# Flamingo-style gated block on one Trainium2 core: the router projection with the gate stationary and the token columns moving

## The reference

```python
# cross part: k = v = ctx, q = layernorm(x), heads of 8 channels
kv = einsum('bhil,bhjl->bijhl', k_, v_)
y = irfft(rfft(kv, 2L) * rfft(ssm_kernel, 2L))[..., :L]     # causal convolution of length 1024
out = einsum('bijhl,bhil->bjhl', y + kv * D, q_)
x = x + tanh(g_xattn[0]) * out
# expert part, n = layernorm(x), tokens are the 4096 rows of 1024
scores = softmax(n @ G)            # G is (1024, 8): the router projection
value, indices = top_k(scores, 2)
x = x + tanh(g_ffn[0]) * sum over the 2 experts of value * (down(silu(gate n) * up n) + lora)
```

## Time and profile before

| what | value |
|---|---|
| median of 3 runs | 1568.64 us (1567.76 to 1572.28) |
| the profiled execution | 1570.3 us, span 1568.5 us |
| mean granted TensorE clock | 0.965 of full |
| TensorE busy | 1426.0 us, 91% |
| TensorE weight loads busy | 1380.1 us, 88% |
| VectorE busy | 1148.1 us, 73% |
| ScalarE busy | 774.6 us, 49% |
| GpSimd busy | 1177.9 us, 75% |

### The profile page before, as it was taken

How to read it: one execution, slowest core, us unless ns; L and a number is a source line. 1 busy time by engine, 2 the same in 40 slices (tenths; PEclk the granted TensorE clock), 3 DMA queues, 4 the chain that set the end, 5 groups by cost and what they waited for, 6 DMA issues and landing times. The chain is left out here.

```text
span 1568.5 us, 33155 instructions
## 1 busy us (share of the span) xinstructions
PE 1426.0 (91%) x10482; PEld 1380.1 (88%) x10483; DVE 1148.1 (73%) x1913; ACT 774.6 (49%) x1359; POOL 1177.9 (75%) x765
## 2 busy tenths in 40 slices
PE   4999999999999999999999999545998988989994
PEld 4999999999999999999999999445988877888883
DVE  3999999999999999999999999582444444444442
ACT  5665656656665565566657565102333333333331
POOL 6989888898988989889898887043656566565664
PEclk9999999999999999999999999657999999999997
DMA  5766667676676766767666675164999999999996
GB/s 193 229 201 226 203 216 223 208 231 201 215 225 207 227 200 223 217 207 229 207 221 211 209 227 187 53 196 109 174 224 222 199 214 229 196 215 230 170 171 88
DMA packets 124431, 314.97 MB, mean 201 GB/s; under 512 B 26160, under 2 KB 26672, under 8 KB 124400
## 3 DMA queue, kind: packets, MB, share of 16 engines
q1 hardware_dynamic: 93728, 239.83, 49.6%
q0 software_dynamic: 30672, 74.75, 24.4%
HBM read 215.37 MB, written 100.73 MB: 202 GB/s over the span
## 5 line engine op out<-in xcount | busy, mean ns | idle before, releaser
L532 DVE TENSOR_REDUCE oT<-z 128x128 f32<-128x1280 f32 x256 | 380.6, 1487 | 7.8
L633 PE MATMUL Y<-kvhi,t_hi 128*128 128x288 f32 x1280 | 382.6, 299 | 0.0
L634 PE MATMUL Y<-kvlo,t_hi 128*128 128x288 f32 x1280 | 377.8, 295 | 0.0
L635 PE MATMUL Y<-kvhi,t_lo 128*128 128x288 f32 x1280 | 377.1, 295 | 0.0
L1081 POOL DMA_INDIRECT out<-made,dest x142 | 222.3, 1566 | 164.6 <-DMA out<-made,dest 115.4
L307 POOL TENSOR_TENSOR kvlo<-kv,kvhi 128x1152 fp32r<-128x1152 f32 x128 | 340.7, 2683 | 0.0
L290 POOL TENSOR_TENSOR kv<-cT 128x768 f32<-128x768 f32 x128 | 236.5, 1847 | 8.4 <-DMA cT<-in_c 8.4
L634 PEld LDWEIGHTS Y<-kvlo,t_hi 128*128 128x128 f32 x1280 | 241.0, 188 | 0.0
L635 PEld LDWEIGHTS Y<-kvhi,t_lo 128*128 128x128 f32 x1280 | 241.0, 188 | 0.0
L633 PEld LDWEIGHTS Y<-kvhi,t_hi 128*128 128x128 f32 x1280 | 240.7, 188 | 0.0
L515 DVE TENSOR_TENSOR z<-Y,qT 128x512 f32<-128x512 f32 x256 | 176.9, 691 | 50.6 <-PE Y L635 41.8
(11 more groups left out here) (162 smaller groups left out, 3337.9 us busy)
## 6 DMA issues: line engine op xcount, KB each, us to landing
cT<-in_c SPq DMA_DIRECT2D x32, 768.0 KB, 8.1
t_hi<-khi SPq DMA_DIRECT2D x64, 384.0 KB, 3.8
t_lo<-klo SPq DMA_DIRECT2D x64, 384.0 KB, 5.0
u_hi<-kshi SPq DMA_DIRECT2D x64, 320.0 KB, 5.9
u_lo<-kslo SPq DMA_DIRECT2D x64, 320.0 KB, 6.9
x_nat<-in_x SPq DMA_DIRECT2D x32, 512.0 KB, 4.2
out<-x_new SPq DMA_DIRECT2D x32, 512.0 KB, 4.9
normed<-n SPq DMA_DIRECT2D x32, 512.0 KB, 7.6
```

What stands on the lines that cost most here:

```text
L532: nc.vector.tensor_reduce(oT[p][:, 2 * r:2 * r + 2, h * IB:(h + 1) * IB], view(z[s][:], [[ZC, 2], [2, IB], [2 * IB, ZS], [1, 2]]), AX.XY, ...
L633: nc.tensor.matmul(out, w_hi[:, w], m_hi[:, c, :], start=start, stop=False)
L634: nc.tensor.matmul(out, w_hi[:, w], m_lo[:, c, :], start=False, stop=False)
L635: return nc.tensor.matmul(out, w_lo[:, w], m_hi[:, c, :], start=False, stop=stop)
```

## The change

The gate becomes the stationary operand: 128 x 16, its high and its low 8 columns. The high and the low part of the transposed tokens lie beside each other in `n2_parts` and move together, 256 columns for each of the 8 blocks of the model dimension. The result is 16 x 256 in the first bank of XP: rows are gate columns, columns are high and low tokens. ScalarE copies it into `gated`, whose other 112 rows have been set to zero once. A new step on TensorE, `turn`, transposes the two halves of `gated` into the second bank of XP, and VectorE sums for each token and expert the four terms. The product of the two low parts, which the old form leaves out, is now in the sum. `turn(i - 2)` stands in TensorE's list after `shared(i, 1)`, and VectorE's `take_lr` moves from before to after the fourth `total` of head 0.

```diff
-        n2_hi, n2_lo = sb("n2_hi", [P, NC, P], F32R), sb("n2_lo", [P, NC, P], F32R)
+        n2_parts = sb("n2_parts", [P, NC, 2, P], F32R)
-        p_small = sb("p_small", [P, E])
+        gated = sb("gated", [P, 2 * P])
...
                 def take_small(i):
                     eng.wait_ge(ag_ready, i + 1)
-                    if not (isinstance(i, int) and i < 1):
-                        eng.wait_ge(lr_done, i)
-                    nc.scalar.copy(p_small[:], XP[:, E:2 * E]).then_inc(small_done, 1)
+                    if isinstance(i, int) and i < 1:
+                        eng.wait_ge(gated_zero, 1)
+                    else:
+                        eng.wait_ge(turned, i)
+                    nc.scalar.copy(gated[0:2 * E, :], XP[0:2 * E, 0:2 * P]).then_inc(small_done, 1)
...
                 def take_lr(i):
-                    eng.wait_ge(ag_ready, i + 1)
+                    eng.wait_ge(turned, i + 1)
                     at = slice(i, i + 1) if isinstance(i, int) else bass.ds(i, 1)
                     to = logits[:, at, :].rearrange("p o n -> p (o n)")
-                    eng.wait_ge(small_done, i + 1)
-                    nc.vector.tensor_tensor(to, XP[:, 0:E], p_small[:], ALU.add).then_inc(lr_done, 1)
-
-
+                    nc.vector.tensor_reduce(to, view(XP[:], [[1, E], [P, 2], [E, 2]], HALF), AX.XY, ALU.add).then_inc(lr_done, 1)
+
+
+                nc.vector.memset(gated[:], 0.0).then_inc(gated_zero, 1)
...
                     multiply(i, p, 0, 3)
+                    total(i, p, 0, 3)
                     if not (isinstance(i, int) and i < 2):
                         take_lr(i - 2)
-                    total(i, p, 0, 3)
...
                     for c in range(NC):
 
-                        nc.tensor.matmul(XP[:, 0:2 * E], n2_hi[:, c, :], ag_parts[:, c].rearrange("p o n -> p (o n)"),
-                                         start=c == 0, stop=False)
-                        mm = nc.tensor.matmul(XP[:, 0:E], n2_lo[:, c, :], ag_parts[:, c, 0, :], start=False, stop=c == NC - 1)
+                        mm = nc.tensor.matmul(XP[0:2 * E, 0:2 * P], ag_parts[:, c].rearrange("p o n -> p (o n)"),
+                                              n2_parts[:, c].rearrange("p o n -> p (o n)"), start=c == 0, stop=c == NC - 1)
                     mm.then_inc(ag_ready, 1)
+
+                def turn(i):
+                    eng.wait_ge(small_done, i + 1)
+                    for half in range(2):
+                        mm = nc.tensor.transpose(XP[:, HALF + half * P:HALF + (half + 1) * P],
+                                                 gated[:, half * P:(half + 1) * P], ident[:])
+                    mm.then_inc(turned, 1)
...
                     conv(i, 0, 3)
                     shared(i, 1)
+                    if not (isinstance(i, int) and i < 2):
+                        turn(i - 2)
                     conv(i, 1, 0)
...
                 project(NT - 2)
+                turn(NT - 2)
                 transpose_n2(NT - 1, 1)
                 project(NT - 1)
+                turn(NT - 1)
```

More of the change, by code:

```diff
@@ L179, in attend @@
         lr_done = sem("lr_done")
+        turned = sem("turned")
+        gated_zero = sem("gated_zero")
         w_in, whi_done, wlo_done, w_out = sem("w_in"), sem("whi_done"), sem("wlo_done"), sem("w_out")
@@ L442, in high_n2 @@
                         eng.wait_ge(ag_ready, i)
-                    nc.scalar.copy(n2_hi[:], XP[:].rearrange("p (c n) -> p c n", c=NC)).then_inc(n2hi_done, 1)
+                    nc.scalar.copy(n2_parts[:, :, 0, :], XP[:].rearrange("p (c n) -> p c n", c=NC)).then_inc(n2hi_done, 1)
                 def take_small(i):
                     eng.wait_ge(ag_ready, i + 1)
-                    if not (isinstance(i, int) and i < 1):
-                        eng.wait_ge(lr_done, i)
-                    nc.scalar.copy(p_small[:], XP[:, E:2 * E]).then_inc(small_done, 1)
+                    if isinstance(i, int) and i < 1:
[3 more added lines that the diff above has]
+                    nc.scalar.copy(gated[0:2 * E, :], XP[0:2 * E, 0:2 * P]).then_inc(small_done, 1)
                 eng.wait_ge(k_sum, 1)
@@ L555, in low_n2 @@
                     eng.wait_ge(n2hi_done, i + 1)
-                    nc.vector.tensor_tensor(n2_lo[:], XP[:].rearrange("p (c n) -> p c n", c=NC), n2_hi[:].bitcast(F32),
+                    nc.vector.tensor_tensor(n2_parts[:, :, 1, :], XP[:].rearrange("p (c n) -> p c n", c=NC), n2_parts[:, :, 0, :].bitcast(F32),
                                             ALU.subtract).then_inc(n2lo_done, 1)
                 def take_lr(i):
-                    eng.wait_ge(ag_ready, i + 1)
+                    eng.wait_ge(turned, i + 1)
                     at = slice(i, i + 1) if isinstance(i, int) else bass.ds(i, 1)
                     to = logits[:, at, :].rearrange("p o n -> p (o n)")
-                    eng.wait_ge(small_done, i + 1)
-                    nc.vector.tensor_tensor(to, XP[:, 0:E], p_small[:], ALU.add).then_inc(lr_done, 1)
+                    nc.vector.tensor_reduce(to, view(XP[:], [[1, E], [P, 2], [E, 2]], HALF), AX.XY, ALU.add).then_inc(lr_done, 1)
+                nc.vector.memset(gated[:], 0.0).then_inc(gated_zero, 1)
                 nc.vector.memset(epsc[:], EPS)
```

## The result

The changed kernel takes 1552.51 us (median of 4 runs, 1550.58 to 1554.7) against 1570.14 (4 runs) for the kernel before: 17.6 us less, ratio 0.989, 95% interval 0.9865 to 0.9915. In a second comparison on another occasion it was 1551.8 against 1567.37, 15.6 us less, ratio 0.9899 (0.9882 to 0.9915). Forecast were 1551 us and a gain of 17.6.

A forecast was written before the change was run, and what follows sets the result against it. TensorE's instruction list was taken to bound each 30.28 us turn: 1.79 - 0.95 - 0.22 = 0.62 us saved, 0.57 taken. Thirty turns (17.1) plus tail (0.5) give 17.6 us, so 1551 us; range 1547 to 1563.

The forecast's parts named there:

- TensorE sets the turn, and what it gives up comes off: Loop turn of 30.28 us is TensorE's instruction list; time removed at the projection shortens it, up to VectorE's slack.
- Projection of before, 1.79 us, priced by its loads: Old projection on TensorE: 16 matmuls at 0.112 us each, set by bringing in 128 stationary columns.
- Projection after, 0.95: New projection on TensorE: eight matmuls of 256 moving columns at 0.119 us, 0.95 us in all; bounds 0.85 and 1.06.
- Two transposes, 0.22: Two transposes added on TensorE in every turn cost 0.22 us; upper bound 0.44.
- ScalarE's copy hidden, 0.365: ScalarE's copy of the projection grows from 0.166 to 0.365 us, over 2 us before the transposes need it.
- The cap at the transposes of n2: Transposes of n2 wait for VectorE's later logits reduction, capping the saving at 0.59 us a turn; 0.57 taken.
- Rival 1: Logits reduction or its semaphore delays the transposes of n2: saving 0.30 a turn, 1559 us; chance 0.18 with half drain.
- main case: Whole kernel: saving of 0.45 to 0.62 us a turn, 1549 to 1556 us, chance 0.62.
- The signs that were named: Expected in the changed profile: matmul distance 0.12, turn 29.7, form 128*128, VectorE's wait 0.25, n2 transposes' wait at most 0.1.
- Rival 2: Form change drains TensorE into and out of the projection, 0.54 us a turn: 1566 us, half 1558; full drain shares 0.10.
- Rivals 3 and 4: 3: small loads not hidden under matmuls, 1626 us, chance 0.10. 4: VectorE becomes the bound, 1568 us, shares 0.10.
- Turns and tail: 30 loop turns at 0.57 give 17.1 us; behind the loop, last-but-one projection 0, last one 0.5.

The follow-up runs named there:

- logits first: Changed kernel with VectorE's reduction of the logits moved back in front of the fourth reduction of oT: 1548.39 us, ratio 0.985; again 1546.31 us, 0.9865.
- wide gate: Changed kernel with the gate's 16 columns repeated to a stationary operand of 128 columns, same 256 moving columns: 1553.39 us, ratio 0.9887.
- moved tail: Logits first, plus group 30's projection and transposes moved before the last transposition of oT: 1541.02 us, ratio 0.984; again 1544.35 us, 0.9853.

## Why the prediction was right, point by point

- **TensorE sets the turn, and what it gives up comes off.** Right, where TensorE does not stand. Edits of its list moved the turn by what the sum of distances says: -0.896 for eight matmuls fewer, +0.221 for two transposes with the logits first, and +0.50 for a wait of 0.65, of which 0.17 filled the other wait. Where TensorE stood, the same two transposes added only 0.022.
- **Projection of before, 1.79 us, priced by its loads.** The 1.79 is right; half as many of the same kind take 0.89. That the loads set it is argued and not shown.
- **Projection after, 0.95.** Measured 0.93, 0.117 a matmul; the line through 272 and 512 columns gave 0.119. The lower bound of 0.107 is not that line's slope without a fixed part, as the text says (0.44 x 256 = 0.114), but nothing hung on it. That a load of 128 columns would also be hidden: right (wide gate, 0.119).
- **Two transposes, 0.22.** Measured 0.22 in place and 0.221 in the turn. The upper bound of 0.44 was not needed.
- **ScalarE's copy hidden, 0.365.** Measured 0.34; it is covered by the 21 matmuls, and TensorE stands for 0.65 us without them.
- **The cap at the transposes of n2.** The mechanism was right and its size too small. I put the loss at 0.05 (0.57 taken of 0.62); the wait is 0.17 and the restart 0.02, so that 1.79 - 0.93 - 0.22 - 0.19 = 0.45 remain, 0.441 by the turns. The step that was mis-sized: "the old addition at 523.72 goes away, so the fourth reduction starts there". Before, the product ahead of it gave way to the addition after 0.20 us and this to the reduction after 0.11; now the product gives way to the reduction after 0.31 (516.95 to 517.26). The kernel says why: `total` waits for `z_done`, which the product's end raises, and in both kernels the reduction starts 0.03 after that end (523.80 to 523.83, 517.23 to 517.26). The addition waits for nothing that the product makes, so it had run in a gap that is there anyway, and taking it away freed nothing: 0.10 us. This could have been read before the change. VectorE's timeline of the kernel before has the product that the earlier trace rows leave out, and the pair ahead of it, which has no addition between and the same 0.31:

```profile
520.74 0.28 DVE L521 TENSOR_TENSOR z<-Y,qT 128x128 f32<-128x128 f32 x1
521.05 1.49 DVE L532 TENSOR_REDUCE oT<-z 128x128 f32<-128x1280 f32 x1
...
523.52 0.28 DVE L521 TENSOR_TENSOR z<-Y,qT 128x128 f32<-128x128 f32 x1
```

The increment took 0.15 instead of 0.13, and TensorE arrived 0.02 earlier than reckoned, which adds to the wait. Rival 1 had the place and the kind. With the reduction at 0.18, as taken, the saving of 0.441 a turn lies just below the 0.45 to 0.62 of the main case and just above the 0.30 to 0.41 of rival 1.
- **The signs that were named.** Met: the distances, the missing step of 0.21, the two transposes at 0.22 and no wait for the copy. Missed: the turn (29.84, not 29.7), the form (128*16, not 128*128), VectorE's wait (0.11, not 0.25), and the wait of the transposes of n2 (0.17, not at most 0.1). The sign of rival 1, a row of waits with more than 5 us, is there for their weight loads: 5.1 us in 24 turns.
- **Rival 2, a drain at the change of form.** No price of it shows, though the form in the row did change, against what I forecast: 128*16. The same stretch takes 1.20 us with the narrow form and 1.22 without it, where rival 2 put 0.27 on each change. On the rule of the Trainium skill's page on TensorEngine Tiling, Key Properties, the trace does not agree for this case, a narrow stationary operand of float32r between wide ones. Either such an operand is no tiling mode of its own, or its drain costs nothing here; the runs can't tell, and other forms were not tried.
- **Rivals 3 and 4.** Loads stayed under the matmuls, and VectorE let 0.896 through.
- **Turns and tail.** 30 x 0.57 = 17.1 was forecast, 30 x 0.441 = 13.2 measured. The tail was put at 0.5, of which the last projection gave 0.8 (1008.23 to 1012.27 before, 993.08 to 996.33 after), and the last but one, put at nothing because "TensorE waits for ScalarE anyway", gave 1.5: it was ScalarE that waited for this projection. Together 2.3. The two errors, -3.9 and +1.8, partly cancel: 15.5 from turns and tail together, against 17.6 on record. That the first comparison gave just 17.6 is luck: the second one gave 15.6, the interval of the first reaches from 13 to 21 us, and parts of the kernel that the change does not touch vary by more than the 2 us that are left.

## What to carry to other kernels

Where a loop is filled by one engine's list, price a matmul by the distance to the next one's start, not by its duration. Here it was 0.112 us with 8 or 16 moving columns, and 0.117 with 256, so that the same work in half as many, fuller matmuls nearly halved the cost, while at 256 moving columns a narrower stationary operand gave next to nothing. Follow each semaphore of a step that you move: a cheap instruction put behind a long one, 1.4 us later on an engine that is not the bound, held the engine that is, for 0.19 us of the 0.63 that the list had given up, and moving it back got them. At the ends of a loop look again at who waits for whom, and at the clock. Behind the loop the projections of before ran at a granted clock of 0.50 and took some 3.4 us each instead of 1.8, and the one that seemed hidden in TensorE's wait held ScalarE, because of ScalarE's own order of work. Halving it gave 1.5 us; taking it out of the way altogether, in the kernel with the moved tail, gave 0.4 to 0.65 more.

## What the runs showed of the hardware

- The distance of eight matmuls with 256 moving float32r columns is 0.117 us with 16 stationary columns and 0.119 with 128, although the load itself takes 97 ns in the one and 198 ns in the other.
- Going from 128*128 to 128*16 and back between matmuls in a stream showed no cost: 1.20 us over the projection and its two edges, against 1.22 with 128*128 throughout.
- Matmuls with 128 stationary and 8 or 16 moving columns follow each other at 0.112 us at full clock and at 0.214 at a granted clock of 0.50 (and the projection of group 30 above).
- A short VectorE instruction can be free if the one behind it waits for the end of the one ahead of it anyway: the time from the product to the long reduction behind it was 0.31 us with the addition in between (0.20 and 0.11, the product started at 523.52) and 0.31 without it; with the logits first it is again 0.19 + 0.12, which the timeline of that kernel shows:

```profile
514.99 0.28 DVE L525 TENSOR_TENSOR z<-Y,qT 128x128 f32<-128x128 f32 x1
515.18 0.18 DVE L567 TENSOR_REDUCE logits<-XP 128x32 f32 x1
515.30 1.49 DVE L536 TENSOR_REDUCE oT<-z 128x128 f32<-128x1280 f32 x1
```

- A wait of 0.17 us of TensorE can be absent from the PE rows of the list of waits. It shows as a distance, between two starts that are 0.13 us apart elsewhere, and as a row of the weight loads without a releaser.
